# Softmax sums of two 16-head attentions: from the exponentials' accumulator and two folds, in place of products with ones

## The chip, the cores and the metric

The kernel is one program on one core of a Trainium2 chip. The metric is the device time of that program in microseconds. TensorE (PE in the profile) multiplies, VectorE (DVE) and ScalarE (ACT) read its results from PSUM, POOL (GpSimd) works on SBUF alone, and SyncE (SP) issues DMAs. Every engine takes its own queue in order; semaphores order the engines among each other.

## The reference, cut to what matters

Five parts follow each other on x of 32 batch entries x 128 rows x 128 columns: an 8-head cross-attention, a feed-forward part that also yields inputs of a router, a 16-head cross-attention (`l1`), a 16-head causal self-attention (`mla`), and a mixture of experts. The change touches the two 16-head attentions, with 8 columns per head:

```
q, k, v = projections of the normalized input (l1: k and v of the context, 120 rows)
scores = q @ k.T / sqrt(8) + mask
a = softmax(scores, axis=-1)          # exp(scores - max) / sum(exp(scores - max))
out = (a @ v) @ w_o                   # added to the input
```

Beside l1 the kernel also runs a search over the router's logits (the 512 largest of 1536 per batch entry): 16 rounds, each of which counts how many keys lie above three trial values and takes one base-4 digit from the counts.

## The kernel before

`attention16` is called once for l1 (K = 120 keys) and once for mla (K = 128). One step serves one batch entry, 32 steps in all, software-pipelined: `steps` runs each engine's `body(n, par, k)`, and in one body the engine works on entries n - 2 to n + 1. The order of work on each engine is the order of the calls in its body. No planner stands behind it.

For one entry: POOL centres and normalizes (`centre`, `norm_input`, in mla also `norm_output`); TensorE transposes (`turn_input`, L1466) and projects (`project_qkv`, L1473 to L1476); ScalarE copies q and k (`copy_q` L1557, `copy_k` L1563), VectorE v; POOL spreads q into four slots (`spread_q`, L1734); TensorE writes the bias and the scores of all 16 heads into four PSUM banks (`scores`, L1489 and L1494). Heads 0 to 7 (half a) are taken by `max_a` (VectorE, L1609) and `exp_a` (ScalarE, L1570), eight exponentials with the maximum as bias. Heads 8 to 15 (half b) are taken by `max_b` (L1616), `shift_b` (L1625), which subtracts the maximum, and one exponential over all eight, `exp_b` (L1577). The probabilities are transposed in four groups (`turn_group`, L1504), copied to SBUF by ScalarE (groups 0 and 2) and VectorE (1 and 3) (`copy_group`, L1447), and multiplied with V and with a tile ONE that holds ones (`multiply_v`, L1514 and L1517), each as four products on 32 columns of the array. So the second product leaves each row's sum in PSUM, repeated for the 8 columns of its head and already turned. VectorE inverts it (`invert_sums`, L1634, 128x128), scales (`scale_out`, L1640), TensorE projects (`project`, L1524), and VectorE adds the result to x (`add_projection`, L1647) and takes statistics.

TensorE's body ends with `scores(n + 1)` and `turn_group(n, 0)`; VectorE's ends with `max_a(n + 1)`, and ScalarE's with `exp_a(n + 1)`.

A round of the search is laid over two steps of l1. ScalarE tries three values (`try_number` L1583: trial 0 after exp_a of the even step, 1 and 2 in the odd step around copy_group 0); TensorE sums the counts over partitions (`total_trials`, L1530); VectorE reads the digit (`read_digit`, L1658) and makes the next trials (`next_trials`, L1666 to L1668). After eight rounds `second_half` sets up the other eight.

Of the kernel before, what the change touches and what calls it, by code (L numbers as in the profile page):

```python
# [52 lines left out]
def mega_kernel(nc, x_in, ctx_in, ctxT_in, keep_in, qk_mask_in, cols_in, lnow_in, lnob_in, wq0_in, wkv0_in, wo0_in,  # L53
# [3 lines left out]
    with ctx:  # L57
        def sb(name, shape, dt=F32, stack=ctx):
# [40 lines left out]
        shared = dict(V=[sb(f"V{i}", [P, 4 * (P + 8)]) for i in range(2)], ONE=sb("ONE", [P, 4 * (32 + 8)]),  # L99
                      own_rows=sb("own_rows", [P, 16]), row_pairs=sb("row_pairs", [P, 2, 4]), own_slots=sb("own_slots", [P, 4]),  # L100
# [704 lines left out]
def make_constants(pool, router, shared, zeroed, selected):  # L805

    same_entry, earlier = router["same_entry"], router["earlier"]
    own_rows, pairs, own_slots, ONE, bias = (shared[k] for k in ("own_rows", "row_pairs", "own_slots", "ONE", "mla_bias"))
    pool.memset(same_entry[:, :], 0.0).then_inc(zeroed, 1)
    pool.memset(earlier[:, :], 0.0).then_inc(zeroed, 1)  # L810
    pool.memset(own_rows[:, :], 1.0).then_inc(zeroed, 1)
    pool.memset(bias[:, 0, :], 0.0).then_inc(zeroed, 1)
    pool.memset(ONE[:, :], 0.0).then_inc(zeroed, 1)
    for q in range(2):
        pool.memset(shared["V"][q][:, :], 0.0)
    pool.wait_ge(zeroed, 5)
    for slot in range(4):
        pool.memset(ONE[:, slot * 40:slot * 40 + 8], 1.0)
# [427 lines left out]
def search_tiles(sb):  # L1246
# [7 lines left out]
                offsets=sb("offsets", [P, 3]), bias=sb("trial_bias", [P, 3]), below4=sb("below4", [P, 1]), per_unit=sb("per_unit", [P, 1]),  # L1254
# [32 lines left out]
def attention16(nc, kind, l1, psum, XI, XO, stats6, mean, rstd, mhalf, small, ident, ident_bf, cols,  # L1287
# [5 lines left out]

    H, HD = 16, 8
# [3 lines left out]
    with ExitStack() as sems, ExitStack() as st:  # L1298
# [5 lines left out]
        V, ONE, own_slots, joined = (shared[k] for k in ("V", "ONE", "own_slots", "joined"))  # L1304
# [7 lines left out]
        with nc.Block() as block:  # L1312
# [27 lines left out]
            def _(dve):  # L1340
# [5 lines left out]
                if router:  # L1346
# [3 lines left out]
                    first_trials(dve, t)  # L1350
                    dve.wait_ge(logits_done, 1)
# [40 lines left out]
        r_sums = sb("r_sums", [P, P])  # L1392
# [21 lines left out]
        multiplied = [sem(f"multiplied{g}") for g in range(4)]  # L1414
        sums_inverted = sem("sums_inverted")
        out_scaled = sem("out_scaled")
        projected = sem("projected")
# [8 lines left out]
        halved = sem("halved")  # L1426

# [29 lines left out]
        with nc.Block() as block:  # L1457
            @block.tensor
            def _(pe):
# [47 lines left out]
                def multiply_v(n, par, g):  # L1507
                    if there(n):
# [10 lines left out]
                        mm.then_inc(multiplied[g], 1)  # L1519

# [5 lines left out]
                def total_trials(k, n):  # L1526
                    if round_there(k):
                        wait(pe, tried, k + 1)
                        wait(pe, out_scaled, n + 1)
# [3 lines left out]
                def body(n, par, k):  # L1533
                    turn_group(n - 1, 1 - par, 3)
                    turn_input(n + 1)
                    if router and par == 0:
                        total_trials(k - 1, n - 2)
# [7 lines left out]
                    multiply_v(n - 1, 1 - par, 3)  # L1545
                    scores(n + 1, 1 - par)
# [5 lines left out]
            def _(act):  # L1552
# [12 lines left out]
                def exp_a(n, par):  # L1565
                    if there(n):
                        wait(act, max_a_taken, n + 1)
                        wait(act, turned[1], n - 1)
                        for h in range(8):
                            e = act.activation(probs[par][:, h, :], psum[:, h // 4, (h % 4) * K:(h % 4 + 1) * K], ACT.Exp,  # L1570
                                               bias=n_max[par][:, h:h + 1])
                        e.then_inc(a_exp_done, 1)

# [5 lines left out]
                def try_number(k, d):  # L1579
                    if round_there(k):  # L1580
                        if d == 0:
                            wait(act, trials_ready, k)
                        c = act.activation(search["tried"][:, d, :], search["key"][:, :], ACT.Sign, bias=search["bias"][:, d:d + 1],  # L1583
# [569 lines left out]
```

## Time and profile before

| | before |
|---|---|
| median of 3 runs | 1364.15 us (1363.6 to 1365.42) |
| the profiled execution | 1362.49 us |
| its span, first to last instruction | 1360.4 us |
| mean granted TensorE clock | 0.967 |
| TensorE busy | 1226.8 us, 90% |
| VectorE busy | 941.5 us, 69% |
| ScalarE busy | 795.5 us, 58% |
| POOL busy | 577.5 us, 42% |

The busy times are means over five parts with different limits, so they say little about one of them. A matmul's end is modelled, and neighbouring matmuls overlap, so TensorE's share is not its load. Most of what follows goes by single steps: the distance from one instruction to the same one a step later.

### The profile page before, as it was taken

To read this page: it belongs to the slowest core of one execution; us is meant where nothing else is said; L and a number is where in the kernel's file an instruction comes from. 1 tells how busy PE (TensorE), PEld (TensorE's weight loads), DVE (VectorE), ACT (ScalarE), POOL (GpSimd) and SP (SyncE) were. 2 spreads that over 40 slices of the span, in tenths; PEclk is the share of its full clock that TensorE was granted. 3 is DMA by queue.
4 is the path that set the end of the run, shared out by engine and by line. 5 is a ranking of instruction groups with operands and counts; after the bars stand their busy time and mean duration, and the time that the engine had idled before them with its cause. 6 is when DMAs were issued, how large, how long until landed. Compare 5 with 4: busy or idle time off the path is not lost. (4 is left out here: it accounts for less than half of the span.)

```text
span 1360.4 us, 37961 instructions
## 1 busy us (share of the span) xinstructions
PE 1226.8 (90%) x13719; PEld 877.9 (65%) x13719; DVE 941.5 (69%) x2042; ACT 795.5 (58%) x2101; POOL 577.5 (42%) x613
## 2 busy tenths in 40 slices
PE   1799999999999986969888888499999979999996
PEld 0466666666666653437766677378888857777775
DVE  6466766767767754758989889489999966334341
ACT  1588788787787761226776676356666633333332
POOL 3587665665665645022222222343333324333443
PEclk9899999999999997969999999789999989999998
DMA  8000000000000000000000000200000000000000
GB/s 213 11 2 1 0 0 0 0 0 0 0 0 0 0 1 1 0 8 10 9 8 8 8 7 7 64 2 1 0 0 0 1 2 9 9 8 8 8 8 17
DMA packets 22740, 14.71 MB, mean 11 GB/s; under 512 B 6378, under 2 KB 21610, under 8 KB 22540
## 3 DMA queue, kind: packets, MB, share of 16 engines
q1 hardware_dynamic: 22520, 13.75, 3.8%
q8 instruction: 43, 0.70, 0.2%
q14 instruction: 29, 0.24, 0.1%
q10 hardware_dynamic: 148, 0.01, 0.0%
HBM read 11.66 MB, written 2.10 MB: 10 GB/s over the span
## 5 line engine op out<-in xcount | busy, mean ns | idle before, releaser
L694 POOL TENSOR_TENSOR r_norm<-ssm,mhalf 128x24 f32<-128x24 f32 x32 | 134.8, 4213 | 161.8 <-DVE ssm L599 161.8
L1929 ACT ACTIVATE moe_hid<-psum 128x512 f32<-128x512 f32 x128 | 76.3, 597 | 136.7 <-PE psum L1863 136.6
L537 ACT ACTIVATE l_probs<-psum,l_n_max 128x248 f32<-128x248 f32 x256 | 117.0, 480 | 57.5 <-DVE l_n_max L617 57.5
L2087 POOL TENSOR_TENSOR moe_acc<-moe_acc,moe_prod 128x512 f32<-128x512 f32 x64 | 81.4, 1272 | 146.4 <-DVE moe_prod L2043 146.4
L1873 PEld LDWEIGHTS psum<-w,moe_hid 128*128 128x128 f32 x1024 | 123.1, 192 | 26.8 <-issue 26.5
L2043 DVE TENSOR_TENSOR moe_prod<-psum,moe_combine 128x512 f32<-128x512 f32 x64 | 44.2, 691 | 134.9 <-PE psum L1873 134.8
L1873 PE MATMUL psum<-w,moe_hid 128*128 128x128 f32 x1024 | 123.4, 275 | 0.0
L1863 PE MATMUL psum<-moe_moe_hT,w 128*128 128x512 f32 x256 | 121.6, 602 | 0.0
L1734 POOL TENSOR_TENSOR l_QX<-l_qT,own_slots 128x512 f32<-128x512 f32 x32 | 33.3, 1040 | 184.0 <-ACT l_qT L1557 184.0
L1734 POOL TENSOR_TENSOR mla_QX<-mla_qT,own_slots 128x512 f32<-128x512 f32 x32 | 33.3, 1040 | 135.5 <-ACT mla_qT L1557 135.5
L701 POOL TENSOR_TENSOR qkn<-qk,r_norm 128x1536 f32<-128x1536 f32 x32 | 88.3, 2761 | 2.5
L644 DVE TENSOR_TENSOR outT<-psum,r_spread 128x256 f32<-128x256 f32 x64 | 26.8, 419 | 78.8 <-PE psum L445 73.3
L617 DVE TENSOR_REDUCE l_n_max<-psum 128x4 f32<-128x992 f32 x64 | 76.2, 1191 | 6.6 <-PE psum L401 2.6
L1504 PE MATMUL psum<-ident,mla_probs 128*128 128x128 f32 x512 | 77.8, 286 | 0.3 <-ACT mla_probs L1570 0.2
L1504 PE MATMUL psum<-ident,l_probs 128*120 128x128 f32 x512 | 76.8, 284 | 0.6 <-ACT l_probs L1570 0.5
L1570 ACT ACTIVATE mla_probs<-psum,mla_n_max 128x128 f32<-128x128 f32 x256 | 69.5, 383 | 8.6 <-DVE mla_n_max L1609 5.1
L636 DVE COPY l_probsT<-psum 128x512 f32<-128x512 f32 x64 | 44.3, 692 | 43.0 <-PE psum L422 43.0
L1570 ACT ACTIVATE l_probs<-psum,l_n_max 128x120 f32<-128x120 f32 x256 | 67.6, 377 | 8.1 <-DVE l_n_max L1609 8.1
L1447 ACT COPY mla_probsT<-psum 128x512 f32<-128x512 f32 x64 | 39.2, 613 | 48.6 <-PE psum L1504 48.6
L129 POOL TENSOR_TENSOR rstd<-small,mhalf 128x7 f32<-128x7 f32 (+2 forms) x17 | 28.0, 1646 | 93.5 <-DVE small L1342 53.4
L1863 PEld LDWEIGHTS psum<-moe_moe_hT,w 128*128 128x128 f32 x256 | 45.0, 194 | 34.9 <-issue 34.4
L508 ACT COPY qk<-psum 128x512 f32<-128x512 f32 (+1 forms) x96 | 55.2, 629 | 20.0 <-PE psum L349 12.3
(309 smaller groups left out, 3422.3 us busy)
## 6 DMA issues: line engine op xcount, KB each, us to landing
X<-x_in SPq DMA_DIRECT2D x8, 256.0 KB, 4.8
out_dram<-moe_acc SPq DMA_DIRECT2D x32, 64.0 KB, 1.5
CT<-ctx_in SPq DMA_DIRECT2D x8, 240.0 KB, 5.9
l_cT<-ctxT_in SPq DMA_DIRECT2D x32, 60.0 KB, 1.8
w<-w_in SPq DMA_DIRECT2D x1, 1024.0 KB, 5.3
wm<-wm_in SPq DMA_DIRECT2D x1, 768.0 KB, 4.4
wp<-wp_in SPq DMA_DIRECT2D x1, 768.0 KB, 6.5
wkv<-wkv_in SPq DMA_DIRECT2D x1, 512.0 KB, 5.1
```

Source lines behind the costliest of these rows:

```text
L508: act.copy(qk[0:rows, part, :], psum[0:rows, bank, :]).then_inc(s[copied], 1)
L537: e = act.activation(probs[u][:, h, :], psum[:, 2 * u + h // 2, (h % 2) * K:(h % 2 + 1) * K], ACT.Exp, bias=n_max[u][:, h:h + 1], accum_ou ...
L617: dve.tensor_reduce(n_max[u][:, :].rearrange("p (c j) -> p c j", c=2), psum[:, 2 * u:2 * u + 2, 0:2 * K].rearrange("p c (j k) -> p c j k", ...
L694: pool.tensor_tensor(r_norm[:, :], ssm[:, :], mhalf[:, 0:3 * H], ALU.pow).then_inc(s["norm_inverted"], 1)
L701: pool.tensor_tensor(qkn[:, :, :].rearrange("p a (h d) -> p (a h) d", d=HD), qk[:, :, :].rearrange("p a (h d) -> p (a h) d", d=HD), r_norm ...
L1504: tr = pe.transpose(psum[0:K, 4 + g % 2, j * P:(j + 1) * P], probs[par][:, 4 * g + j, :], ident[:, :])
L1570: e = act.activation(probs[par][:, h, :], psum[:, h // 4, (h % 4) * K:(h % 4 + 1) * K], ACT.Exp, bias=n_max[par][:, h:h + 1])
L1734: pool.tensor_tensor(QX[par][:, :, :], qT[:, :].unsqueeze(1).broadcast_to([P, 4, P]), own_slots[:, :].unsqueeze(2).broadcast_to([P, 4, P]) ...
L1863: pe.matmul(psum[:, 2 + i % BANKS, :], w1[:, e, half * P:(half + 1) * P], hT[par][:, :], start=True, stop=True).then_inc(hidden[i], 1)
L1873: mm = pe.matmul(psum[:, 5 + e % 2, b * D:(b + 1) * D], hid[i % RING][:, b * P:(b + 1) * P], w2[:, i, :], start=(half == 0), stop=(half == ...
L1929: act.activation(hid[i % RING][:, :], psum[:, 2 + i % BANKS, :], ACT.Silu).then_inc(activated[i], 1)
L2087: pool.tensor_tensor(a[:, :, :], a[:, :, :], prod[e % 2][:, :, :], ALU.add).then_inc(summed[e], 1)
```

## The change

- The products with ONE and the tile are gone.
- Half a: each of the eight exponentials of `exp_a` also writes its row sum (`accum_out`). Half b: POOL adds the two halves of each row, then the two halves of that (`fold_b`), and VectorE reduces the remaining quarter (`sum_b`).
- The reciprocal works on 128x16 sums. POOL widens it to 128x128 (`widen_inverses`), TensorE transposes it (`turn_inverses`, ahead of `scores`), ScalarE copies it out of PSUM (`copy_inverses`, behind `exp_b`), and `scale_out` multiplies with the copy.
- POOL's body: spread_q and widen_inverses first, then centring and norms for an entry one step further ahead, then fold_b.
- Search pieces: trial 0 and 1 in the odd step between copy_inverses and copy_group 0, trial 2 in the even step ahead of exp_b; total_trials behind the last products; read_digit ahead of scale_out; next_trials on POOL as four instructions; second_half behind max_a.

```diff
@@ TensorE
                         for tile in range(4):
-                            pe.matmul(psum[32 * tile:32 * tile + 32, 6, 0:P], V[par][0:K, g * P + 32 * tile:g * P + 32 * tile + 32],
+                            mm = pe.matmul(psum[32 * tile:32 * tile + 32, 6, 0:P], V[par][0:K, g * P + 32 * tile:g * P + 32 * tile + 32],
                                       probsT[0:K, g, tile, :], start=(g == 0), stop=(g == 3), skip_group_check=True)
-                        for tile in range(4):
-                            mm = pe.matmul(psum[32 * tile:32 * tile + 32, 6, P:2 * P], ONE[0:K, 32 * g:32 * g + 32],
-                                           probsT[0:K, g, tile, :], start=False, stop=(g == 3), skip_group_check=True)
+                def turn_inverses(n):
+                        wait(pe, inverses_widened, n + 1)
+                        pe.transpose(psum[:, 6, P:2 * P], r_wide[:, :], ident[:, :]).then_inc(inverses_turned, 1)
                 def body(n, par, k):
                     turn_group(n - 1, 1 - par, 3)
                     turn_input(n + 1)
-                    if router and par == 0:
-                        total_trials(k - 1, n - 2)
                     project(n - 2)
...
                     multiply_v(n - 1, 1 - par, 3)
+                    if router and par == 0:
+                        total_trials(k - 1)
+                    turn_inverses(n - 1)
                     scores(n + 1, 1 - par)
                     turn_group(n, par, 0)
@@ ScalarE
+                        wait(act, sums_inverted, n - 1)
                         for h in range(8):
                             e = act.activation(probs[par][:, h, :], psum[:, h // 4, (h % 4) * K:(h % 4 + 1) * K], ACT.Exp,
-                                               bias=n_max[par][:, h:h + 1])
+                                               bias=n_max[par][:, h:h + 1], accum_out=sums[par][:, h:h + 1])
+                def copy_inverses(n):
+                        wait(act, inverses_turned, n + 1)
+                        wait(act, out_scaled, n)
+                        act.copy(r_spread[:, :], psum[:, 6, P:2 * P]).then_inc(inverses_copied, 1)
                     copy_k(n + 1, 1 - par)
+                    if router and par == 0:
+                        try_number(k - 1, 2)
                     exp_b(n, par)
+                    copy_inverses(n - 1)
                     if router and par == 1:
+                        try_number(k, 0)
                         try_number(k, 1)
                     copy_group(act.copy, act, n, 0)
-                    if router and par == 1:
-                        try_number(k, 2)
                     exp_a(n + 1, 1 - par)
-                    if router and par == 0:
-                        try_number(k, 0)
@@ VectorE
-                        dve.reciprocal(r_sums[:, :], psum[:, 6, P:2 * P]).then_inc(sums_inverted, 1)
+                        dve.tensor_reduce(sums[par][:, 8:16], quarters[:, :, :], AX.X, ALU.add).then_inc(b_summed, 1)
...
+                        wait(dve, a_exp_done, n + 1)
+                        wait(dve, b_summed, n + 1)
+                        wait(dve, inverses_widened, n)
+                        dve.reciprocal(r_sums[:, :], sums[par][:, :]).then_inc(sums_inverted, 1)
...
-                        dve.tensor_tensor(outT[:, :], psum[:, 6, 0:P], r_sums[:, :], ALU.mult).then_inc(out_scaled, 1)
+                        dve.tensor_tensor(outT[:, :], psum[:, 6, 0:P], r_spread[:, :], ALU.mult).then_inc(out_scaled, 1)
                 def body(n, par, k):
                     copy_input(dve, n + 1)
                     copy_group(dve.tensor_copy, dve, n - 1, 3)
-                    if router and par == 0:
-                        read_digit(k - 1, n - 2)
                     add_projection(n - 2)
+                    sum_b(n - 1, 1 - par)
                     max_b(n, par)
+                    invert_sums(n - 1, 1 - par)
                     take_stats(n - 2)
-                    if router and par == 0:
-                        next_trials(k - 1)
                     shift_b(n, par)
                     copy_group(dve.tensor_copy, dve, n, 1)
                     copy_values(dve.tensor_copy, dve, n + 1, 1 - par)
-                    invert_sums(n - 1)
+                    if router and par == 0:
+                        read_digit(k - 1, n - 1)
                     scale_out(n - 1)
                     max_a(n + 1, 1 - par)
+                    if router and par == 0 and isinstance(k, int) and k == ROUNDS:
+                        second_half()
@@ POOL
+                def next_trials(k):
+                        wait(pool, digit_read, k + 1)
...
+                        pool.tensor_tensor(t["below"][:, :], t["below4"][:, :], t["digit4"][:, :], ALU.subtract).then_inc(below_made, 1)
...
+                def fold_b(n, par):
+                        wait(pool, b_exp_done, n + 1)
+                        wait(pool, b_folded, n)
+                        pool.tensor_tensor(halves[:, :, :], probs[par][:, 8:16, 0:K // 2], probs[par][:, 8:16, K // 2:K], ALU.add).then_inc(b_halved, 1)
+                        wait(pool, b_halved, n + 1)
+                        wait(pool, b_summed, n)
+                        pool.tensor_tensor(quarters[:, :, :], halves[:, :, 0:K // 4], halves[:, :, K // 4:K // 2], ALU.add).then_inc(b_folded, 1)
+                def widen_inverses(n):
+                        wait(pool, sums_inverted, n + 1)
+                        wait(pool, inverses_turned, n)
+                        r = r_sums[:, :].rearrange("p (s t) -> p t s", t=4).unsqueeze(3).broadcast_to([P, 4, 4, HD])
+                        pool.tensor_tensor(r_wide[:, :].rearrange("p (t s d) -> p t s d", t=4, s=4), r,
+                                           shared["one"][:, :].unsqueeze(2).unsqueeze(3).broadcast_to([P, 4, 4, HD]), ALU.mult).then_inc(inverses_widened, 1)
                 def body(n, par, k):
-                    centre(n + 1)
-                    norm_output(n + 1)
-                    norm_input(n + 1)
-                    spread_q(n + 1, 1 - par)
+                    spread_q(n + 1, 1 - par)
+                    widen_inverses(n - 1)
+                    centre(n + 2)
+                    norm_input(n + 2)
+                    norm_output(n + 2)
+                    fold_b(n, par)
+                    if router and par == 0:
+                        next_trials(k - 1)
                     later_scales(n)
```

## Rows read from the trace of the kernel before

**Rows 1.** Windows, mla: busy us by engine (records), granted clock, DMA share, GB/s

```profile
975.00:1000.00 25.00, 25.00 (x512) 20.46 (x509) 24.84 (x42) 16.52 (x45) 8.62 (x16) 1.00 0.00 0
```

**Rows 2.** Timeline, VectorE, mla: start us, us, engine, line, operation, tiles

```profile
985.00 1.22 DVE L1609 TENSOR_REDUCE mla_n_max<-psum 128x8 f32<-128x1024 f32 x1
...
988.53 1.21 DVE L1625 TENSOR_TENSOR mla_probs<-psum,mla_n_max 128x1024 f32<-128x1024 f32 x1
...
990.55 0.95 DVE L1634 RECIPROCAL mla_r_sums<-psum 128x128 f32<-128x128 f32 x1
991.53 0.29 DVE L1640 TENSOR_TENSOR mla_outT<-psum,mla_r_sums 128x128 f32<-128x128 f32 x1
991.74 1.23 DVE L1609 TENSOR_REDUCE mla_n_max<-psum 128x8 f32<-128x1024 f32 x1
```

**Rows 3.** Timeline, VectorE, l1: outT of three steps

```profile
699.29 0.29 DVE L1640 TENSOR_TENSOR l_outT<-psum,l_r_sums 128x128 f32<-128x128 f32 x1
...
707.80 0.29 DVE L1640 TENSOR_TENSOR l_outT<-psum,l_r_sums 128x128 f32<-128x128 f32 x1
...
715.09 0.29 DVE L1640 TENSOR_TENSOR l_outT<-psum,l_r_sums 128x128 f32<-128x128 f32 x1
```

**Rows 4.** Timeline, all engines, one step of mla

```profile
999.74 2.17 ACT L1570 ACTIVATE mla_probs<-psum,mla_n_max 128x128 f32<-128x128 f32 x8
...
1001.75 0.32 ACT L1557 ACTIVATE mla_qT<-psum 128x128 f32<-128x128 f32 x1
...
1002.01 1.21 DVE L1625 TENSOR_TENSOR mla_probs<-psum,mla_n_max 128x1024 f32<-128x1024 f32 x1
1002.15 1.04 POOL L1734 TENSOR_TENSOR mla_QX<-mla_qT,own_slots 128x512 f32<-128x512 f32 x1 [4.32 <-ACT mla_qT L1557]
1002.38 0.34 ACT L1563 COPY mla_kT<-psum 128x128 f32<-128x128 f32 x1
...
1003.15 0.40 POOL L1714 TENSOR_TENSOR mla_centred<-X,mean 128x128 f32 x1
...
1003.25 1.06 ACT L1577 ACTIVATE mla_probs<-mla_probs 128x1024 f32<-128x1024 f32 x1 [0.53 <-DVE mla_probs L1625]
...
1003.62 0.43 PE L1489 MATMUL psum<-mla_bias,ident_bf 32*32 32x512 bf16 x16
...
1005.23 1.22 DVE L1609 TENSOR_REDUCE mla_n_max<-psum 128x8 f32<-128x1024 f32 x1
```

**Rows 5.** Timeline, POOL to TensorE, early in mla

```profile
897.70 0.40 POOL L1721 TENSOR_TENSOR mla_zn<-mla_centred,mla_scale 128x128 f32<-128x128 f32 x1
...
898.15 0.33 PE L1466 MATMUL psum<-ident,mla_zn 128*128 128x128 f32 x1 [0.47 <-POOL mla_zn L1721]
...
898.32 0.39 PE L1524 MATMUL psum<-mla_wo,mla_outT 128*128 128x128 f32 x2
```

**Rows 6.** Timeline, a step of l1 with a search piece

```profile
741.39 1.15 DVE L1609 TENSOR_REDUCE l_n_max<-psum 128x8 f32<-128x960 f32 x1
...
742.57 2.12 ACT L1570 ACTIVATE l_probs<-psum,l_n_max 128x120 f32<-128x120 f32 x8 [0.21 <-DVE l_n_max L1609]
...
744.53 0.75 ACT L1583 ACTIVATE tried<-key,trial_bias,per_unit 128x384 bf16<-128x384 f32 x1
...
745.22 0.32 ACT L1557 ACTIVATE l_qT<-psum 128x128 f32<-128x128 f32 x1
```

**Rows 7.** Groups of instructions: busy us, mean ns, idle before

```profile
L1517 PE MATMUL psum<-mla_probsT,ONE 128*32 128x128 f32 x1024 | 51.6, 273 | 0.0
```

**Rows 8.** Timeline, ScalarE, first attention: exponentials with an accumulator

```profile
302.84 0.49 ACT L537 ACTIVATE l_probs<-psum,l_n_max 128x248 f32<-128x248 f32 x1
303.20 0.22 ACT L537 ACTIVATION_READ_ACCUMULATOR l_probs<-psum,l_n_max 128x1 f32 x1
303.29 0.49 ACT L537 ACTIVATE l_probs<-psum,l_n_max 128x248 f32<-128x248 f32 x1
```

**Rows 9.** Windows, TensorE alone, l1's longest stall

```profile
738.00:740.00 2.00, 0.36 (x18) 1.00 0.00 0
```

More of the change, by code:

```diff
@@ L98, in mega_kernel @@
         search = search_tiles(sb)
-        shared = dict(V=[sb(f"V{i}", [P, 4 * (P + 8)]) for i in range(2)], ONE=sb("ONE", [P, 4 * (32 + 8)]),
-                      own_rows=sb("own_rows", [P, 16]), row_pairs=sb("row_pairs", [P, 2, 4]), own_slots=sb("own_slots", [P, 4]),
+        shared = dict(V=[sb(f"V{i}", [P, 4 * (P + 8)]) for i in range(2)],
+                      own_rows=sb("own_rows", [P, 16]), one=sb("one", [P, 1]), row_pairs=sb("row_pairs", [P, 2, 4]), own_slots=sb("own_slots", [P, 4]),
                       l1_bias=sb("l1_bias", [P, 4, C], BF16), mla_bias=sb("mla_bias", [P, 4, P], BF16), l1_mask=l1_weights["mask"],
@@ L807, in make_constants @@
     same_entry, earlier = router["same_entry"], router["earlier"]
-    own_rows, pairs, own_slots, ONE, bias = (shared[k] for k in ("own_rows", "row_pairs", "own_slots", "ONE", "mla_bias"))
+    own_rows, pairs, own_slots, bias = (shared[k] for k in ("own_rows", "row_pairs", "own_slots", "mla_bias"))
     pool.memset(same_entry[:, :], 0.0).then_inc(zeroed, 1)
@@ L811, in make_constants @@
     pool.memset(own_rows[:, :], 1.0).then_inc(zeroed, 1)
+    pool.memset(shared["one"][:, :], 1.0)
     pool.memset(bias[:, 0, :], 0.0).then_inc(zeroed, 1)
-    pool.memset(ONE[:, :], 0.0).then_inc(zeroed, 1)
     for q in range(2):
         pool.memset(shared["V"][q][:, :], 0.0)
-    pool.wait_ge(zeroed, 5)
-    for slot in range(4):
-        pool.memset(ONE[:, slot * 40:slot * 40 + 8], 1.0)
+    pool.wait_ge(zeroed, 4)
     n = 0
@@ L1350, in _ @@
                     first_trials(dve, t)
+                    dve.memset(t["four"][:, :], 4.0)
                     dve.wait_ge(logits_done, 1)
@@ L1391, in attention16 @@
         probsT = sb("probsT", [P, 4, 4, P])
-        r_sums = sb("r_sums", [P, P])
+        sums = [sb(f"sums{i}", [P, H]) for i in range(2)]
+        r_sums = sb("r_sums", [P, H])
+        halves = sb("halves", [P, 8, K // 2])
+        quarters = sb("quarters", [P, 8, K // 4])
+        r_wide = sb("r_wide", [P, P])
+        r_spread = sb("r_spread", [P, P])
         outT = sb("outT", [P, P])
@@ L1735, in spread_q @@
                                            own_slots[:, :].unsqueeze(2).broadcast_to([P, 4, P]), ALU.mult).then_inc(q_spread, 1)
+                def next_trials(k):
+                    if round_there(k):
+                        t = search
+                        wait(pool, digit_read, k + 1)
+                        wait(pool, trials_ready, k)
+                        if isinstance(k, int) and k == ROUNDS:
+                            wait(pool, halved, 4)
+                        pool.tensor_tensor(t["below"][:, :], t["below4"][:, :], t["digit4"][:, :], ALU.subtract).then_inc(below_made, 1)
+                        wait(pool, below_made, k + 1)
+                        pool.tensor_tensor(t["bias"][:, :], t["offsets"][:, :], t["below"][:, :].broadcast_to([P, 3]), ALU.add).then_inc(bias_made, 1)
+                        wait(pool, bias_made, k + 1)
+                        pool.tensor_tensor(t["below4"][:, :], t["below"][:, :], t["four"][:, :], ALU.mult).then_inc(below4_made, 1)
+                        wait(pool, below4_made, k + 1)
+                        pool.tensor_tensor(t["per_unit"][:, :], t["per_unit"][:, :], t["four"][:, :], ALU.mult).then_inc(trials_ready, 1)
                 def later_scales(n):
```

59 lines of the change are left out of this document (32 added, 27 removed).

## The prediction

> **What bounds the kernel now.** I read the granted clock and the page first, then the stretches by window, then single steps of the two 16-head stages in the timeline, because the diff touches nothing else. The first of them (l1) runs from about 597 to 863 us, the second (mla) from about 875 to 1104, 32 steps each. In mla the window row shows TensorE busy for all of its 25 us and VectorE for 24.84 [rows 1]. TensorE's figure flatters it: matmuls overlap, and their ends are modelled. VectorE's instructions really stand end to end: from one max_a to the next (985.00 to 991.74) is 6.74 us without a hole [rows 2]. So mla is bound by VectorE's queue, at 6.74 us a step. In l1 the starts of outT are 8.51 and 7.29 us apart in turn, a pair of 15.80 or 7.90 a step [rows 3].
>
> A second chain runs nearly as long, and the reader should see it before pricing anything. From the start of max_a(n): the maximum until ScalarE's eight exponentials start 1.25 (999.74, and max_a a period before 1005.23, at 998.49), the exponentials 2.01, qT 0.32 and 0.08 to POOL's start, spread_q, then the bias matmul at 1003.62 and the next max_a 1.61 after that [rows 4]. The chain without waits is 1.25 + 2.01 + 0.40 + 1.04 + 0.10 + 1.61 = 6.41 (0.10 from spread_q's end to the bias, my estimate from the 0.05 of [rows 5]). VectorE wins now by 0.33 only. In l1 a search piece stands inside that chain on every second step: exponentials at 742.57, a try at 744.53, qT at 745.22 [rows 6]. With it the chain is 1.18 + 1.96 + 0.69 + what follows, and that is the 7.29.
>
> **What leaves.** In each step 16 products with ONE. They are 1024 records (32 a step) of 51.6 us together in mla, 1.6 a step [rows 7]; I estimate 0.9 of queue time, since consecutive groups overlap. TensorE has no queue that must end there: in mla VectorE sets the step, and after the change neither is first (below). I count nothing in the steady step for it: multiply_v(3) ends about half a microsecond before widen does. Bounds: 0 and 0.9, the latter had the products stood last ahead of the scores. The 128x128 reciprocal leaves VectorE: 0.98 from its start to scale_out [rows 2]. Six search instructions leave VectorE every second step of l1, and no try stands between exp_a and copy_q any more: 0.69 off the chain there, every second step [rows 6].
>
> **What comes, off the path.** VectorE gets sum_b, 256 elements: between a quarter of max_a's 1.22 (0.31) and the whole; I take 0.33, nearest the quarter. It gets a reciprocal of 16 values in place of 128: between 0 and 0.98, I take 0.2 since an eighth of the values is left. VectorE's own work in mla becomes 6.74 - 0.98 + 0.53 = 6.29. scale_out now also waits for copy_inverses, which ScalarE does behind exp_b: exp_b starts 1.24 after shift_b (1002.01 to 1003.25) and takes 1.06, the copy about 0.32 as qT does [rows 4]; scale_out comes at about shift_b + 2.6, where today it comes at + 3.00 (988.53 to 991.53). From scale_out to shift_b the row gives 0.21 + 3.53, now + 0.53 = 4.27. That loop is 6.85, no bound of mine but the second longest. POOL gets fold_b: halves at about spread_q's 1.04 (both 512 elements) and quarters between 0.40 and 1.04, I take 0.7. With spread_q, widen, and the three 128-wide ones (0.40 each [rows 4]) POOL holds about 4.6 to 5 us. fold_b starts after exp_b, ends about 9.2 after max_a, and the next sum_b wants it at about 9.9. The moved next_trials, four tiny POOL instructions, ends before the next spread_q (about 12). centre and the norms run a step ahead. These edits cost nothing as long as the step is above 6.85; with that cover gone a late fold_b would cost what it is late, and ahead of VectorE's max_b and shift_b it would reach exp_b too.
>
> **What comes, on the path.** Follow the chain again from max_a.
> - Each of the eight exponentials of exp_a gets accum_out, which makes a second instruction, the read. In the first attention such a read starts at 303.20 and the next exponential at 303.29: 0.09 in the queue, though its row says 0.22 [rows 8]. Eight cost 0.72. Bounds: 0 (wholly hidden) and 8 x 0.22 = 1.8 (not hidden at all, which the rows speak against). I take 0.72, since it is read from the same pair of instructions on the same engine.
> - POOL's queue is spread_q(n+1), then widen_inverses(n-1). widen's input is long there (its reciprocal stands two VectorE instructions ahead of shift_b). So it starts when spread_q is through, 1.00 after it began (1002.15 to 1003.15), and takes 0.40 as the 128-element centre does [rows 4]. Bounds: 0.2 and 1.04, the 512-element form.
> - TensorE's queue is turn_inverses(n-1), then scores(n+1). So the scores, which today need only spread_q, now stand behind widen and a transpose. POOL's end to TensorE is 0.05 (898.10 to 898.15), and the next matmul comes 0.17 later at 898.32 [rows 5]; with the waits ahead of the bias I take 0.25. Bounds 0.17 and 0.4.
>
> The Trainium skill's "GPSIMD Engine Reference", section 7, says that GPSIMD reads cost about half more per element when the step in SBUF is over 8 bytes, and widen reads r_sums in steps of 16. By it widen would be about 0.5, an estimate, and the total 6 us more; no row here shows such a read.
>
> **The step after.** mla: 1.25 + (2.01 + 0.72) + 0.40 + 1.00 + 0.40 + 0.05 + 0.25 + 1.61 = 7.69. On every second step spread_q starts a little later after qT; I round to 7.74. Minus 6.74 is +1.00 a step, over 31 steps from max_a to max_a +31.0 us.
> l1: 1.18 (741.39 to 742.57) + (1.96 + 0.72) + 0.40 + 1.00 + 0.40 + 0.05 + 0.25 + 1.61 = 7.57, with the same rounding 7.60. Even steps have total_trials ahead of turn_inverses on TensorE; its try runs behind copy_k (0.63 after qT [rows 4]) for 0.7, so it comes about as late as widen: 0.14 on such a step, bounds 0 and 0.69. Average 7.67 against 7.90: -0.23, over 30 steps -6.9 us. The odd step's two tries stand ahead of copy_0 and end at about 7.6, before turn_group 0 is there; they fit, with 0.2 to spare.
> Fill and drain: behind the last step fold, sum, inverse, widen, transpose, copy follow each other where products and one reciprocal stood: 0.8 for each stage, +1.6; in the fill the products removed are short of that again. The second_half of the search costs VectorE the same stall in either kernel.
> Sum: 31.0 - 6.9 + 1.6 = +25.7. On the profiled execution, 1362.49 us (span 1360.4), this is 1388.2. The median of the runs before is 1.66 above that execution, so 1389.9, and I say 1390. What a measurement here can tell from no change is 0.2%, 2.7 us.
>
> **Rivals.**
> Not slower: the read of the accumulator hides behind the exponential it follows. For it: the exponential's own row is longer than the distance to the next (0.49 against 0.36), so there is overlap to use. Against: the rows were taken with that overlap in place, and the next exponential still starts 0.09 after the read's start and 0.45 after the one before it [rows 8]. Then mla is 7.02 (+0.28, +8.7 us), l1 6.95 (-0.95, -28.5), with +1.6 a total of -18, 1346. It decides from where the two stages' average falls by 0.41 a step, that is, reads under 0.04 each. 11 in 100 with all ways of ending not slower.
> POOL dear: widen's four-level pattern costs like the 512-element form, 1.04. Then each of 61 steps gets 0.64 more, +39: 1429. The rows give broadcast inputs 0.40 at 128 elements and nothing with short runs of 8. 9 in 100.
> The clock falls: TensorE loses products and waits longer in each step. For it: the mean granted clock is 0.967, so it does fall to its lower level of 1.2 GHz somewhere. Against: between 738 and 740, in l1's longest stall, TensorE was busy for 0.36 of 2 us, and the granted clock stayed 1.00, that is 2.4 GHz [rows 9]. Were it to fall in every step, the 1.61 from bias to max_a would grow towards twice that, up to +1.6 a step or +98: 1488 at most from this term, and 1440 if in half the steps. 6 in 100. The Trainium skill's "TensorE: Matmul & The Clock Gate", Part 4, says that a transpose doesn't count as busy for this clock the way a product does; the change takes away products and adds a transpose, so by it this rival is likelier. The mla stage before runs 16 transposes of probabilities in each step at 1.00, so the trace does not bear it out so far.
>
> **How the numbers follow.** The forecast, 74 in 100; its own range 1372 to 1408, from reads of 0.05 instead of 0.09 (-20), widen at 0.2 (-12, not both) up to widen at 0.6 and TensorE's hand-over at 0.4 (+20). The range over the cases, 1364 to 1420, leaves out the better part of the not-slower case, the upper end of POOL dear, and the clock: 2 in 10. Slower by over 0.2%: 0.74 + 0.09 + 0.06 = 0.89, of which I leave 0.02 to no change; so slower 0.87, same 0.04, faster 0.09.
>
> **What would show it.** In mla: max_a to max_a near 7.7, with VectorE idle over a microsecond a step, ended by the scores' matmul (L1494 of before); exponentials 0.34 apart, not 0.25; widen starting straight behind spread_q; turn_inverses idle on POOL, and the bias matmul about 0.25 behind it. In l1 the pair 8.51 and 7.29 becomes two nearly equal steps of 7.6 to 7.7. TensorE's clock 1.00 in both. The prediction is wrong if the exponentials keep their distance, if widen runs ahead of spread_q's end, or if scale_out, not the scores, is what the next max_a waits for.

## The result, and the profile after

The kernel after takes 1398.61 us (1394.75 to 1400.09), against 1364.79 for the kernel before beside it: 1.0242 of it [1.0218, 1.0267], slower by 33.8 us. The profiled execution took 1399.29 us with a span of 1395.1, which is 34.7 more than before; the mean granted clock is 0.948 (0.967 before).

Where the span grew is seen best when it is cut at the first and the last max_a of each attention. The kernel before, by windows: us, busy us (records) of PE, PEld, DVE, ACT and POOL, granted clock, DMA share, GB/s.

```profile
605.73:851.51 245.78, 214.16 (x4200) 174.32 (x4201) 217.63 (x419) 167.82 (x491) 57.82 (x93) 0.98 0.04 8
851.51:880.88 29.37, 13.86 (x219) 10.58 (x216) 11.47 (x33) 7.75 (x21) 9.92 (x10) 0.78 0.23 73
880.88:1092.87 211.99, 209.09 (x4168) 171.52 (x4169) 205.65 (x334) 142.28 (x401) 72.66 (x129) 0.97 0.00 1
```

The kernel after, the same cuts, and one stretch of mla as in [rows 1]:

```profile
605.76:854.02 248.26, 212.79 (x3268) 166.14 (x3269) 190.27 (x404) 195.53 (x769) 133.84 (x242) 0.91 0.04 8
854.02:880.03 26.01, 13.64 (x158) 9.96 (x158) 10.23 (x30) 8.81 (x31) 13.75 (x24) 0.76 0.27 81
880.03:1126.73 246.70, 202.90 (x3238) 155.92 (x3239) 193.10 (x364) 170.77 (x679) 144.07 (x218) 0.95 0.00 1
1000.00:1025.00 25.00, 20.69 (x334) 16.00 (x332) 20.59 (x41) 18.41 (x74) 14.20 (x22) 1.00 0.00 0
```

The mla stage grew by 34.7 us, l1 by 2.5; the stretch between them shrank by 3.4, and 0.9 is left for all the rest. In [rows 1] TensorE and VectorE were full; now neither is (20.69 and 20.59 of 25 us). And the clock over l1 is 0.91 where it was 0.98, which the forecast did not have.

One step of mla after, the timeline with all engines (start us, us, engine, line, operation, tiles), which answers to [rows 2] and [rows 4]:

```profile
903.99 1.23 DVE L1635 TENSOR_REDUCE mla_n_max<-psum 128x8 f32<-128x1024 f32 x1 [0.91 <-PE psum L1509]
...
905.25 0.37 ACT L1588 ACTIVATE mla_probs<-psum,mla_n_max 128x128 f32<-128x128 f32 x1
...
905.52 0.19 ACT L1588 ACTIVATION_READ_ACCUMULATOR mla_probs<-psum,mla_n_max 128x1 f32 x1
905.61 0.36 ACT L1588 ACTIVATE mla_probs<-psum,mla_n_max 128x128 f32<-128x128 f32 x1
...
907.64 0.25 DVE L1668 RECIPROCAL mla_r_sums<-mla_sums 128x16 f32<-128x16 f32 x1
...
908.00 0.31 ACT L1574 ACTIVATE mla_qT<-psum 128x128 f32<-128x128 f32 x1
...
908.40 1.04 POOL L1756 TENSOR_TENSOR mla_QX<-mla_qT,own_slots 128x512 f32<-128x512 f32 x1 [3.06 <-ACT mla_qT L1574]
...
909.39 0.40 POOL L1795 TENSOR_TENSOR mla_r_wide<-mla_r_sums,one 128x128 f32<-128x128 f32 x1
...
909.85 0.33 PE L1536 MATMUL psum<-ident,mla_r_wide 128*128 128x128 f32 x1 [0.36 <-POOL mla_r_wide L1795]
910.11 0.43 PE L1504 MATMUL psum<-mla_bias,ident_bf 32*32 32x512 bf16 x16
...
910.51 0.29 DVE L1674 TENSOR_TENSOR mla_outT<-psum,mla_r_spread 128x128 f32<-128x128 f32 x1 [0.55 <-ACT mla_r_spread L1596]
...
911.71 1.23 DVE L1635 TENSOR_REDUCE mla_n_max<-psum 128x8 f32<-128x1024 f32 x1 [0.91 <-PE psum L1509]
```

The chain of the forecast can be read off link by link: 1.26 from max_a to the exponentials, 2.75 for them and their reads (with the reads one exponential starts 0.34 to 0.36 after another), 0.40 from qT to spread_q, 0.99 until widen, 0.46 until the transpose, 0.26 until the bias, 1.60 until max_a. Together 7.72. The reciprocal was ready 1.5 us before widen could use it: what holds widen is POOL's queue, behind spread_q.

The waits of that engine and its neighbours, kernel after, 920 to 1120 (engine, line, what it waited for: us in all, times, longest):

```profile
DVE mla_n_max L1635 <- PE psum L1509: 26.3, 26, 1.9
PE psum L1519 <- ACT mla_probs L1588: 24.5, 25, 1.1
...
DVE mla_outT L1674 <- ACT mla_r_spread L1596: 13.7, 25, 0.6
PE psum L1536 <- POOL mla_r_wide L1795: 9.8, 25, 0.4
```

VectorE waits in every step for the scores, a microsecond. TensorE waits twice: for the end of exp_a, and for widen.

Most steps of mla are 7.72 or 7.80, but five of the 31 are 8.56 to 8.75, each with one of about 8.0 behind it. In l1 a pair is 7.66 and 7.58 at best, and every third step is 8.3 to 8.6, with one of 7.9 or 8.0 behind it. What makes them longer is in the windows of one microsecond, TensorE alone (us, busy, clock), and in two rows of the timeline of the same place:

```profile
640.00:641.00 1.00, 0.14 (x8) 1.00 0.18 39
641.00:642.00 1.00, 0.91 (x16) 1.00 0.08 23
642.00:643.00 1.00, 0.78 (x19) 1.00 0.00 0
643.00:644.00 1.00, 1.00 (x29) 0.82 0.00 0
644.00:645.00 1.00, 1.00 (x28) 0.50 0.06 16
645.00:646.00 1.00, 1.00 (x12) 0.50 0.00 0
646.00:647.00 1.00, 1.00 (x6) 0.50 0.00 0
647.00:648.00 1.00, 1.00 (x10) 0.97 0.00 0
```

```profile
643.43 1.93 PE L1509 MATMUL psum<-l_kT,l_QX 32*128 32x120 f32 x32
...
645.40 1.16 DVE L1635 TENSOR_REDUCE l_n_max<-psum 128x8 f32<-128x960 f32 x1 [1.15 <-PE psum L1509]
```

The granted clock falls from 1.00 to 0.50 (from 2.4 to 1.2 GHz) for about 3.4 us and comes back. TensorE had been busy for 0.14 of a microsecond three microseconds earlier, while it waited for exp_a, and was working when the clock fell. The 32 products of the scores, on the chain, took 1.93 us there; in the step shown above, at 1.00, the 32 of mla took 1.17, and so did 32 of l1 at 748.40, at 1.00 again.

### The profile page after: what moved, and what is told of

Read it like the earlier page. It is cut to its first block and busy times, and to the rows that moved or that the text cites. A ratio compares the mean times of both kernels' runs of the same rounds, so it can differ in the third digit from the quotient of the medians.

```text
span 1395.1 us, 35238 instructions
## 1 busy us (share of the span) xinstructions
PE 1222.6 (88%) x11735; PEld 854.7 (61%) x11735; DVE 899.7 (64%) x2059; ACT 854.1 (61%) x2677; POOL 732.0 (52%) x865
## 5 line engine op out<-in xcount | busy, mean ns | idle before, releaser
L1519 PE MATMUL psum<-ident,mla_probs 128*128 128x128 f32 x512 | 81.4, 296 | 32.2 <-ACT mla_probs L1588 32.0
L1519 PE MATMUL psum<-ident,l_probs 128*120 128x128 f32 x512 | 85.2, 306 | 26.9 <-ACT l_probs L1588 25.6
L1588 ACT ACTIVATE mla_probs<-psum,mla_n_max 128x128 f32<-128x128 f32 x256 | 89.9, 378 | 8.2 <-DVE mla_n_max L1635 5.3
L1588 ACT ACTIVATE l_probs<-psum,l_n_max 128x120 f32<-128x120 f32 x256 | 88.2, 373 | 6.0 <-DVE l_n_max L1635 5.0
L1519 PEld LDWEIGHTS psum<-ident,mla_probs 128*128 128x128 f32 x512 | 59.8, 150 | 49.4 <-ACT mla_probs L1588 40.6
L1519 PEld LDWEIGHTS psum<-ident,l_probs 128*120 128x120 f32 x512 | 62.5, 152 | 43.8 <-ACT l_probs L1588 34.1
```

The costliest lines, as they stand in the source:

```text
L1519: tr = pe.transpose(psum[0:K, 4 + g % 2, j * P:(j + 1) * P], probs[par][:, 4 * g + j, :], ident[:, :])
```

## The experiments

Times are medians, with the ratio to the kernel before in the same rounds. "After" and "before" are the two kernels; line numbers are each kernel's own.

**a1: widen ahead of spread_q.** After, two calls exchanged.

```diff
+                    widen_inverses(n - 1)
                     spread_q(n + 1, 1 - par)
-                    widen_inverses(n - 1)
```

> The changed kernel with widen_inverses ahead of spread_q in POOL's queue. Theory (the chain max_a, exponentials, qT, spread_q, widen, transpose, scores is what a step lasts): spread_q to bias falls from 1.71 us to about 1.14, so the undisturbed mla step goes from 7.76 to about 7.2 us, l1 from 7.62 to about 7.05; 62 steps give -35 us, some 1363 us. Rival (the step is set elsewhere, by scale_out behind exp_b or by POOL's load): steps stay within 0.1 of 7.76 and 7.62, time within 6 us of the changed kernel's 1398.6.

Measured: 1366.11 us, 1.0006 [0.9996, 1.0016], so 32 us of the 34 are gone with one exchange. The step of mla is 7.30, a pair of l1 7.66 and 7.16: 14 and 6 us over the two stages. The other 12 are mostly falls of the clock that are gone, five instead of ten in l1 (steps of 8.5 to 8.8) and none in steady mla; the trace is that of a1's slowest run, at 1371.28. The timeline of a1, mla:

```profile
988.50 1.23 DVE L1635 TENSOR_REDUCE mla_n_max<-psum 128x8 f32<-128x1024 f32 x1 [0.57 <-PE psum L1509]
...
992.21 0.24 DVE L1668 RECIPROCAL mla_r_sums<-mla_sums 128x16 f32<-128x16 f32 x1
...
992.61 0.40 POOL L1795 TENSOR_TENSOR mla_r_wide<-mla_r_sums,one 128x128 f32<-128x128 f32 x1 [2.63 <-DVE mla_r_sums L1668]
...
992.97 1.04 POOL L1756 TENSOR_TENSOR mla_QX<-mla_qT,own_slots 128x512 f32<-128x512 f32 x1
...
994.19 0.43 PE L1504 MATMUL psum<-mla_bias,ident_bf 32*32 32x512 bf16 x16
...
995.80 1.23 DVE L1635 TENSOR_REDUCE mla_n_max<-psum 128x8 f32<-128x1024 f32 x1 [0.51 <-PE psum L1509]
```

Now widen waits for the reciprocal and spread_q for widen: spread_q starts at 992.97, 4.47 after max_a, where in after it started at 4.41. Behind it only the bias is left. So widen and the transpose behind spread_q cost 0.42 to 0.50 a step in mla; they were on the chain as forecast. From the start of spread_q to the bias the forecast had 1.70 with them ahead and 1.14 without; the traces have 1.71 (908.40 to 910.11) and 1.22 (992.97 to 994.19).

**b1: no accumulators.** After, without `accum_out`. The sums of heads 0 to 7 are left out: their eight columns hold 1.0, set once.

```diff
-                                               bias=n_max[par][:, h:h + 1], accum_out=sums[par][:, h:h + 1])
+                                               bias=n_max[par][:, h:h + 1])
...
+                for i in range(2):
+                    dve.memset(sums[i][:, 0:8], 1.0)
```

> The changed kernel without accum_out in exp_a; the sums of heads 0 to 7 are a constant 1.0 instead, which leaves that part of the softmax unnormalized. Theory (each accumulator read costs 0.09 us in the chain): steps 0.72 shorter, mla about 7.04, l1 about 6.9, 62 steps give -44 us, some 1354 us. Rival (the reads hide, or another loop takes over at once at 7.5 or more): at most -15 us.

Measured: 1339.35 us, 0.9807 [0.9792, 0.9823]: 59 us under after. The steps are 7.00 and 7.08 in mla and 6.94 and 6.86 in l1, each 0.72 below after's undisturbed ones, the eight reads at 0.09 exactly. Over 61 steps that is 44 us. The other 15 are mostly the clock. Between 620 and 836 and between 905 and 1073 it is 1.00 in every window of 12 us but one, the stall of second_half (728 to 740, 0.86). b1 has no products with ONE either, so their absence alone does not make the clock fall.

**c1: the products with ONE kept.** After, with the 16 products of each step back in their place. Nothing reads them before the transpose overwrites them.

```diff
+                        for tile in range(4):
+                            mm = pe.matmul(psum[32 * tile:32 * tile + 32, 6, P:2 * P], ONE[0:K, 32 * g:32 * g + 32],
+                                           probsT[0:K, g, tile, :], start=False, stop=(g == 3), skip_group_check=True)
```

> The changed kernel with the 16 products with ones kept in each step, their result unused. More work on TensorE in the same places. Theory of the clock (the granted clock falls for some 3.4 us at a time in the two stages because TensorE lost products, and that costs 17 us): the falls in l1 and mla vanish or become rare, windows at 1.00, -17 us, against which multiply_v(3) now ends about 0.1 to 0.2 behind widen, +6 to +12: about 1390 us, not above 1398. Rival (the falls have another cause, such as the waits behind exp_a in each step): the same falls, and the time 5 to 20 us above the changed kernel's 1398.6.

Measured: 1386.85 us, 1.0157 [1.0142, 1.0172]. With 16 more products in every step the kernel is 12 us faster. After's windows from 700 to 725, and c1's:

```profile
700.00:725.00 25.00, 21.82 (x356) 17.19 (x354) 18.82 (x41) 20.44 (x80) 13.48 (x24) 0.93 0.03 7
```

```profile
700.00:725.00 25.00, 23.45 (x456) 19.03 (x458) 20.51 (x45) 20.67 (x87) 13.20 (x26) 1.00 0.03 7
```

**c2 and c3: other work in TensorE's idle time.** Is it the products, or any work? c2 puts 16 products ahead of `multiply_v(0)`, where TensorE has time; c3 puts eight transposes of the identity there. Neither result is read.

```diff
                             wait(pe, projection_added, n)
+                            for f in range(4):           # c2
+                                for tile in range(4):
+                                    pe.matmul(psum[32 * tile:32 * tile + 32, 6, P:2 * P], ONE[0:K, 32 * f:32 * f + 32],
+                                              probsT[0:K, 0, tile, :], start=(f == 0), stop=(f == 3), skip_group_check=True)
```
```diff
                             wait(pe, projection_added, n)
+                            for f in range(8):           # c3
+                                pe.transpose(psum[:, 6, P:2 * P], ident[:, :], ident[:, :])
```

> The changed kernel with 16 products with ones a step, results unused, put ahead of multiply_v(0), where TensorE then waits for exp_a for 1.3 us; multiply_v itself stays free of them. Theory of the clock (it falls for want of TensorE work in the step, wherever that stands): no falls in steady l1 and mla, steps 7.6 and 7.75 undisturbed, 1382 to 1388 us as with the products in their old places (1386.85). Rival (what counts is that the busy stretch ahead of the scores is longer): falls stay, 1395 to 1400 us.

> The same place and about the same time, 0.9 us a step, but filled with 8 transposes of the identity instead of 16 products, results unused. Theory A (any TensorE work keeps the clock): as the early products, 1382 to 1388 us, no falls. Theory B (a transpose does not count as a product does, which the Trainium skill's page on TensorE and the clock gate says in Part 4): the falls stay as in the changed kernel, windows at 0.93, 1395 to 1400 us.

Measured: c2 1383.68 us, 1.0133 [1.0113, 1.0153]; c3 1383.9, 1.0135 [1.0111, 1.0159]. The windows of c2, then of c3:

```profile
700.00:725.00 25.00, 23.99 (x471) 19.37 (x473) 20.67 (x45) 20.95 (x89) 13.21 (x26) 1.00 0.03 7
```

```profile
700.00:725.00 25.00, 23.97 (x383) 18.66 (x385) 20.66 (x45) 20.86 (x85) 14.04 (x27) 1.00 0.05 10
```

Inside the two stages, past their first steps (between them the clock is low in every run), both hold 1.00 but for one fall, in l1 at second_half's stall (0.60 and 0.69 from 740 to 744), and both have steps of 7.66 to 7.67 and 7.58 to 7.60 in l1 and 7.72 to 7.73 and 7.80 in mla: those of after where nothing disturbs it. So after minus c2 is what the falls cost, about 15 us. Eight transposes serve as well as 16 products.

**e1: accumulators alone.** Before, with `accum_out` into a tile that nothing reads.

```diff
-                                               bias=n_max[par][:, h:h + 1])
+                                               bias=n_max[par][:, h:h + 1], accum_out=sums[par][:, h:h + 1])
```

> The kernel before with accum_out on the eight exponentials as the one addition; its sums are not used, the products with ones and all else stay. Theory (the chain from max_a through the exponentials was 6.41 and VectorE's queue 6.74, so 0.72 more makes the chain the bound): mla 7.1 to 7.2 us a step, +12 to +14 us; l1's pair at least 0.72 longer (the step with the try in the chain), at most 1.44, +11 to +22 us; 1388 to 1401 us. Rival (ScalarE was idle for over a microsecond a step and takes the reads in): mla stays at 6.74, under 1372 us.

Measured: 1392.0 us, 1.02 [1.018, 1.022]: +27 us from the reads alone, with a single fall of the clock, at second_half's stall of 11.36 us. The mla step is 7.47, which is 6.74 + 0.73. From first to last max_a that is 21.2 us in mla, but only 5.0 in l1, where the pair went from 8.51 and 7.29 to 7.88 and 8.02: the step with the try took the 0.73, and the other gave 0.63 back. The expectation had 12 to 14 and 11 to 22, so the total fell into its range by luck. If the chain had had the 0.33 of slack that the forecast gave it, the step would have been 7.1 to 7.2. It had none, and the kernel before shows why. Timeline, ScalarE and TensorE, the step of [rows 4]:

```profile
1001.91 0.64 ACT L1447 COPY mla_probsT<-psum 128x512 f32<-128x512 f32 x1
...
1002.61 0.43 PE L1514 MATMUL psum<-mla_probsT,V 128*32 128x128 f32 x8
1002.85 0.40 PE L1517 MATMUL psum<-mla_probsT,ONE 128*32 128x128 f32 x8
1003.07 0.40 PE L1514 MATMUL psum<-mla_probsT,V 128*32 128x128 f32 x8
1003.29 0.40 PE L1517 MATMUL psum<-mla_probsT,ONE 128*32 128x128 f32 x8
```

Behind the exponentials and qT comes the copy of group 2, behind it the products of groups 2 and 3, and behind these the bias (1003.62). In [rows 4] terms: 1.25 + 2.01 + 0.16 + 0.70 + 1.01 + 1.61 = 6.74, as long as VectorE's queue. These are distances from start to start, which add up to the step whatever the links are; what makes them a full chain is that none idles. The copy ends 0.06 before the products start, and products and bias follow without a gap. The bias waited for the products, not for spread_q.

**e2: the same without the products.** e1 without the products with ONE; the reciprocal is taken of the V products instead, so the sums are left out.

```diff
-                        for tile in range(4):
-                            mm = pe.matmul(psum[32 * tile:32 * tile + 32, 6, P:2 * P], ONE[0:K, 32 * g:32 * g + 32],
...
-                        dve.reciprocal(r_sums[:, :], psum[:, 6, P:2 * P]).then_inc(sums_inverted, 1)
+                        dve.reciprocal(r_sums[:, :], psum[:, 6, 0:P]).then_inc(sums_inverted, 1)
```

> The kernel before with accum_out in exp_a and without the products with ones; the reciprocal reads the V products instead, so the sums are not applied. Theory (with accum_out alone, 7.47 a step in mla, the bound was the loop exponentials, copy of group 2, products of groups 2 and 3 with V and with ones, scores; in the kernel before that loop was 6.74, as long as VectorE's queue, and I had left it out): without the products the loop is about 7.03 and the one through spread_q 7.13, so mla 7.1 to 7.2 a step, -9 to -11 us there, in all 1370 to 1384 us. Rival (the products were never in a bound): mla stays at 7.47, within 4 us of 1392.

Measured: 1389.76 us (1383.08 to 1395.26), 1.0177 [1.0132, 1.0221]. The mla step is 7.15 and 7.24: the products had stood on the chain, for about 0.3. But the total missed the theory's 1370 to 1384 (it lies in the rival's band, whose mla step of 7.47 did not come), since the clock falls in l1, as the windows show, and steps there reach 8.8:

```profile
650.00:675.00 25.00, 19.35 (x289) 14.93 (x289) 18.95 (x36) 17.54 (x66) 5.39 (x9) 0.86 0.03 9
```

Here nothing of the fold, widen or the transpose exists, and e1, the same kernel with products, has one fall there, of 6.8 us at second_half's stall. So in this pair it is the products' leaving that lets the clock fall. It is not enough by itself: e2's clock holds in steady mla, at steps of 7.15 and 7.24, and so does that of a1 there (7.30), and b1 and ab1, without products, have one fall each in l1 and none in mla. Falls outside second_half's stall came only without the products and in the longest steps among such kernels: after (7.62 and 7.76 undisturbed), a1's l1 (7.41) and e2's l1 (7.7 to 7.9). No run parts the length of a step from the waits in it.

**ab1: a1 and b1 together.** The sums of heads 0 to 7 are left out as in b1.

> The changed kernel with widen_inverses ahead of spread_q and without accum_out in exp_a (the sums of heads 0 to 7 are a constant 1.0, so that part stays unnormalized). Theory (with both terms off the chain the next loop shows, VectorE's through exp_b, copy_inverses and scale_out, forecast at 6.85 in mla): mla 6.8 to 6.95 us a step, less than the two single savings together would give (7.76 - 0.46 - 0.72 = 6.58), some 1320 to 1330 us. Rival (no second loop near): the savings add up, mla 6.6 or less, under 1318 us.

Measured: 1345.0 us, 0.9855 [0.9835, 0.9875], with mla steps of 7.08 and 7.23: 6 us slower than b1. Both theories missed it. Timeline of ab1:

```profile
993.15 0.33 ACT L1574 ACTIVATE mla_qT<-psum 128x128 f32<-128x128 f32 x1
...
993.52 0.24 DVE L1668 RECIPROCAL mla_r_sums<-mla_sums 128x16 f32<-128x16 f32 x1
993.85 0.40 POOL L1797 TENSOR_TENSOR mla_r_wide<-mla_r_sums,one 128x128 f32<-128x128 f32 x1 [2.37 <-DVE mla_r_sums L1668]
994.21 1.04 POOL L1758 TENSOR_TENSOR mla_QX<-mla_qT,own_slots 128x512 f32<-128x512 f32 x1
```

qT is ready at about 993.5, but POOL stands in widen's wait for the reciprocal and spreads q at 994.21. With the exponentials shorter the reciprocal comes last, and the order that helped after by 32 us hurts b1.

**d1: the search moved alone.** Before, with after's places for the search pieces and next_trials on POOL; on every second step the reciprocal also waits for total_trials. The core of the edit:

```diff
                     copy_k(n + 1, 1 - par)
+                    if router and par == 0:
+                        try_number(k - 1, 2)
                     exp_b(n, par)
                     if router and par == 1:
+                        try_number(k, 0)
                         try_number(k, 1)
                     copy_group(act.copy, act, n, 0)
-                    if router and par == 1:
-                        try_number(k, 2)
                     exp_a(n + 1, 1 - par)
-                    if router and par == 0:
-                        try_number(k, 0)
```

> The kernel before, with the search pieces alone moved as in the change (tries, total_trials, read_digit, next_trials on POOL, second_half), softmax sums as before; on every second step the reciprocal also waits for total_trials. Theory (in l1 before, the try between exp_a and qT, and the read of the digit behind project, made the pair 15.80 us; VectorE's own work is 6.4 a step): l1 falls to 6.5 to 6.8 us a step, -34 to -43 us, mla unchanged at 6.74: 1322 to 1330 us. Rival (the search's own round trip sets the pair): l1 stays above 7.3, at most -18 us.

Measured: 1345.84 us, 0.9861 [0.9846, 0.9877]: 19 us faster than before, at mla steps of 6.74. The l1 pair went from 8.51 and 7.29 to 7.51 and 6.99. More was expected, and the waits of d1 from 600 to 860 show what held it:

```profile
POOL below L1736 <- DVE totals L1662: 41.0, 16, 10.6
...
PE psum L1470 <- POOL l_zn L1713: 14.6, 15, 5.1
```

POOL stands in next_trials' wait, and the centring of the next entry, which TensorE wants first, is queued behind it.

**d2: d1 with POOL's centring one entry ahead,** as after has it.

```diff
-                    centre(n + 1)
-                    norm_output(n + 1)
-                    norm_input(n + 1)
                     spread_q(n + 1, 1 - par)
+                    centre(n + 2)
+                    norm_input(n + 2)
+                    norm_output(n + 2)
```

> The kernel before with the search pieces moved and, beyond that, POOL's centring and norms one entry ahead behind spread_q, as in the change. Theory (with the search moved, next_trials waited on POOL for the digit and made the next entry's centring, its transpose, zT and q late; that is what kept l1's pair at 14.51): the TensorE wait for zn goes, l1's average falls from 7.26 to 6.7 to 6.95 us, -10 to -17 us against that kernel's 1345.8, some 1332 us; mla stays at 6.74. Rival (VectorE's wait for total_trials sets the pair): less than 4 us from 1345.8.

Measured: 1328.92 us, 0.9739 [0.9716, 0.9762], the l1 pair at 6.99 and 6.71. The stretch from l1's last max_a to mla's first is 25.6 us, where d1 has 28.7. It computes everything and beats before by 36 us and after by 70.

## Why the prediction was right

**The direction and the chain: right.** 1390 (1364 to 1420) was forecast, 1398.6 came, by the mechanism named: the scores stand behind reads, spread_q, widen and a transpose. The undisturbed mla step was 7.74 by the forecast and 7.72 or 7.80 in the trace; l1's was 7.67 on average and came to 7.62. The reads cost 0.72 a step (b1 in both stages, e1 in mla; in l1 of the kernel before they cost 0.05 on average, e1), and widen 0.40 straight behind spread_q. VectorE's idle microsecond, ended by the scores' matmul, is there too. scale_out waits 0.55 but is done 0.9 before max_a, as the second loop of 6.85 would have it. On widen's price the Trainium skill's "GPSIMD Engine Reference", section 7, gave 0.5 by my estimate. The trace has 0.40, the time of centring's contiguous 128 columns, but it does not test that rule: the innermost dimension of widen's read repeats each value eight times, a step of 0, and the step of 16 bytes lies one dimension further out.

**The sum, against c2, whose clock falls but once inside the stages.** First to last max_a: mla 241.43 us, +29.4 (forecast +31.0); l1 239.72, -6.1 (forecast -6.9), with the step of second_half 0.7 longer against its neighbours than before (10.67 against 7.62; 10.29 against 7.90). The one fall of the clock lies there, and none did before; second_half has also moved, and how much of the 0.7 is the fall is not shown. Fill and drain were put at +1.6, a size that came from no row; between the stages the span shrank by 3.5 instead. Most of that is POOL's order: from l1's last projection to mla's first max_a it is 13.9 to 14.0 us in every run that has this order, d2 among them, and 16.9 in before, d1, e1 and e2. Nor was the drain 0.8 longer: from mla's last max_a to its last outT it is 10.5 us before, 10.75 in after and 10.3 in c2. That is +19.8, and 2.7 more lie ahead of l1's first and behind mla's last max_a. So c2's profiled span is 22.6 above before, its median 17.7; the profiled run was c2's slowest, and the runs of before lie between 1362.0 and 1368.0, so closer than about 3 us the sum cannot be read. I had 25.7.

**What failed: "TensorE's clock 1.00 in both".** The rival "the clock falls" had 6 in 100, with falls in half the steps or all. The clock does fall, in l1 every third step and in mla in five of 31. By stage, after is above c2 by 8.5 us in l1 and 5.3 in mla, 14 together (the 8.5 are net: second_half's step is 8.31 in after and 10.67 in c2, and the other 30 steps are 10.9 longer); by the medians' distances to before it is 33.8 - 17.7 = 16. Forecast and rival are both true, the rival at a size that I did not weigh. The total missed by 8.6 us: these 16, less the 8 that the sum was too high, and 0.6 because the kernel before stood at 1364.8 in these rounds. That two errors of opposite sign left 8.6 is luck; the chain of mla, right to 0.06 a step, is not. My evidence [rows 9] was one stall of 2 us in the kernel with the products. It showed that a stall does not lower the clock there; it could not show what a step with fewer matmuls and two waits does. Fewer products alone would not have done it either (b1); what decides stays open.

The Trainium skill's "TensorE: Matmul & The Clock Gate", Part 4, says that a transpose does not count as busy the way a product does. That page made the rival likelier, and the rival came, but not by that rule: with eight transposes in place of 16 products (c3) the clock holds as well and the time is the same.

**What failed without harm: the products "counted at nothing".** They were on a chain as full as VectorE's queue (e1, e2), which my 6.41 passed by: I had followed q's branch and not that of group 2. The forecast survived because after's chain through widen is longer than either. A forecast of e1 by the same working would have been off by 0.3 a step in mla, some 10 us. In after the term itself held: with the products back in their places (c1) the steps of mla are 7.74 and 7.81 against 7.72 and 7.80, the pair of l1 7.82 and 7.60 against 7.66 and 7.58, which is 3 us in all. And the search takes three instructions off VectorE, L1666 to L1668, not six: read_digit stays there. VectorE's queue sets neither stage of after, so nothing hung on it.

**The other rivals.** "Not slower" fell with e1 and b1: the reads are not hidden. "POOL dear" fell with widen's row of 0.40; halves took 1.31 us (forecast 1.04) and quarters 0.73 (0.7), in POOL's slack.

**What the change is made of.** On before, moving the search gains 19 us (d1) and POOL's order behind it another 17 (d2). The accumulators alone cost 27 (e1). Widen behind spread_q costs what a1 gets back, 32, falls of the clock included. These do not add up to 34, since each is measured on another chain.

## What to carry to other kernels

Before pricing an edit, follow every branch that leads to the instruction that the next step waits for, and add each up: two may be full at once, and removing work from one then shows nothing. An instruction that moves to another engine takes its place in that queue, so ask what it stands behind and what stands behind it; here exchanging two POOL instructions gained 32 us in one kernel and cost 6 in its neighbour. When products leave TensorE, look at the granted clock of the result first, and where it falls try other work in TensorE's idle time.

## What was not expected of the hardware

- Work added to TensorE made the kernel faster: 16 products, or eight 128x128 transposes, in every step of 7.7 us, 15 us in all, where the granted clock then stays at 1.00. Neither the busy time in the records nor the longest wait told beforehand which kernel would keep it: from 700 to 725 e1 keeps 1.00 with TensorE busy for 21.22 of 25 us, and after has 0.93 with 21.82 (the records are longer at the lower clock). Nor does the absence of the products tell: b1 has none of them and keeps 1.00 there, busy for 22.95. What decides is left open.
- A fall in after lasts about 3.4 us (e1's one, at second_half, 6.8) and costs the step in which it lies 0.7 to 1.0 us, and the next one 0.2 to 0.4.
- A row of an accumulator's read behind one of these exponentials says 0.19 to 0.25 us, but it takes 0.09 of ScalarE's queue.
